# A schedule change in the last block of a hybrid transformer kernel: scan rows, row parts, scan factors and the last pass

## Chip, core and metric

The kernel runs on one core of one Trainium2 chip. The metric is device time in microseconds (us) of one execution.

## What is computed

The input is x (4 sequences of 512 rows, 256 wide, float32). Eight layers are added to it one after the other. The last three of them are the block in question:

```python
x = x + ffn(layernorm(x))        # silu(x@w_gate) * (x@w_up), the 2 largest of 4 kept, @ w_down
x = x + scan_layer(layernorm(x))
x = x + ffn(layernorm(x))        # the same weights again
# scan_layer, per sequence:
ct = concat([shifted_by_one_row(x), x], -1)
xv = sigmoid(relu(ct @ W_act.T)); re, im = pairs of xv
m = cummax(sqrt(re*re + im*im)); re, im = re / m, im / m
re, im = associative_scan(complex_multiply, (re, im))       # along the 512 rows
out = (stack(re, im) @ W_val.T) * sigmoid(relu(ct @ W_rec.T)) ** 4
```

The feed-forward has 1024 inner columns, worked in chunks of 128 (FC = 8 chunks a pass, B = 4 sequences of NT = 4 tiles of 128 rows).

## The kernel before

The whole block is one function, `feed_forward_and_scan`, with one program for each engine (`@block.tensor`, `@block.scalar`, `@block.vector`, `@block.gpsimd`, `@block.sync`). Engines meet only through semaphores, and each one works through its own list in the order in which it is written.

The work is laid out in slots n = 0 to 72. There are PASSES = 8 passes (feed-forward of the four sequences, then the second feed-forward of the four) of 8 chunks: 64 chunks in slots 0 to 63. In slot n

- TensorE computes `chunk(n)` (12 products: gate, L1735, and up, L1741), then `down(n - 7)` (products with w_down, L1751, summed in two banks of PSUM over a pass), then the jobs of `pe_at[n]`;
- ScalarE computes silu of chunk n (L1859), then the magnitude of chunk n - 1 (L1845), then the jobs of `act_at[n]`. The magnitude of a chunk whose number divides by four waits until VectorE has compared the four before (`ge_done`);
- VectorE does `dve_first[n]`, then `product(n)` (L2015), then a part of the two-of-four selection of a group of four chunks (`select`: part 0, the comparisons, L2024; part 1, the counts, L2030 to L2034; part 2, the masking, L2039, after which `sel_done` lets `down` start on the group), then `dve_at[n]`. The parts fall in slots with n mod 4 = 0, 1, 2; `down` of a new group is in a slot with n mod 4 = 3;
- GpSimd does `pool_at[n]`, the normalising of x (L1877, L1882).

A pass p ends with `added(p)` = 8(p + 1) + 7: ScalarE copies the sum of the down products from PSUM (`down_sum`, L1815) in the slot before it, and VectorE adds that to x (L2047). The scan of sequence b then begins at slot s = 15, 23, 31, 39 (`scan_from(b)`):

- s: VectorE adds and takes the moments, GpSimd normalises ("s");
- s+1: TensorE transposes the normalised rows (`row`, L1681, after `down`), ScalarE copies them to `xs` (L1777);
- s+2: TensorE computes "act" (L1690) when both copies are there, ScalarE relu, tanh, square (L1785 to L1792);
- s+3, s+4: sum of squares, running maximum, root (ScalarE, L1810), reciprocal (`invert`, L1933), `divide` (L1940, two instructions that read z with a stride and write the factors `zz`), first `level` of the scan;
- s+5, s+6: TensorE "rec" (L1699), ScalarE relu, tanh and two squares; s+5 to s+10: VectorE levels, `tree` steps, `fill` (L1953 to L1957);
- s+10: ScalarE copies `totals` (L1821, L1822) when the last tree step is done; s+11: TensorE "out" (L1710); s+13, s+14: VectorE multiplies and adds to x (L1981, L1984), takes moments for the second feed-forward; s+15: its rows ("f") are transposed.

A row of the feed-forward ("f") is cut into a high part (copied by ScalarE, L1775) and a low part (subtracted by VectorE after that copy, L1903, in `dve_at`). Only then is its bank of PSUM free. These rows are in slots 4, 12, 20 and 30, 38, 46, 54. The transposes, act, rec and out products share banks 6 and 7 in turn (`Turns`).

Because the scans are 8 slots apart, slot s+2 of a scan is slot s+10 of the one before. Where two jobs of ScalarE fall in one slot, they stand in the order in which the loop over b appends them: `totals` of b - 1 first, then the jobs of b.

SyncE stores each sequence to `out` when its last add is done (L1666).

Of the kernel before, what the change touches and what calls it, by code (L numbers as in the profile page):

```python
# [19 lines left out]
ALU = mybir.AluOpType  # L20
# [3 lines left out]
P = 128  # L24
B = 4
# [1519 lines left out]
def feed_forward_and_scan(nc, name, g, raw, w_down, scan, out):  # L1545
# [20 lines left out]
    def scan_from(b):  # L1566
        return added(b)

    pe_at, act_at, pool_at, dve_at, dve_first = ([[] for _ in range(SLOTS)] for _ in range(5))
    for p in range(1, B):  # L1570
        pe_at[FC * p - 4] += [("row", "f", p, c) for c in range(DC)]
        act_at[FC * p - 4] += [("row", "f", p, c) for c in range(DC)]
        dve_at[FC * p - 4] += [("row", "f", p, c) for c in range(DC)]
        pool_at[FC * p - 6].append(("normalise", "f", p))
    dve_at[0].append(("stats", "rest"))
    for p in range(PASSES):
        act_at[added(p) - 1].append(("sum", p))
        dve_first[added(p)].append(("add", p))
    for b in range(B):
        s = scan_from(b)  # L1580
        dve_first[s].append(("stats", "s", b))
        pool_at[s].append(("normalise", "s", b))
        pe_at[s + 1] += [("row", "s", b, c) for c in range(DC)]
        act_at[s + 1] += [("row", "s", b, c) for c in range(DC)]
        pe_at[s + 2] += [("act", b, 0), ("act", b, 1)]
        act_at[s + 2] += [("act", b, 0), ("act", b, 1), ("square", b)]
        dve_at[s + 3] += [("sum", b), ("peak", b)]
        act_at[s + 3].append(("root", b))
        dve_first[s + 4].append(("invert", b))
        dve_at[s + 4] += [("divide", b), ("level", b, 1)]  # L1590
        pe_at[s + 5].append(("rec", b, 0))
        act_at[s + 5].append(("rec", b, 0))
        dve_at[s + 5].append(("level", b, 2))
        pe_at[s + 6].append(("rec", b, 1))
        act_at[s + 6].append(("rec", b, 1))
        dve_at[s + 6].append(("level", b, 3))
        dve_at[s + 7] += [("level", b, i) for i in (4, 5, 6)]
        dve_at[s + 8] += [("level", b, 7)] + [("tree", b, d) for d in TREE[:2]]
        dve_at[s + 9] += [("tree", b, d) for d in TREE[2:5]]
        dve_at[s + 10] += [("tree", b, d) for d in TREE[5:]] + [("fill", b)]  # L1600
        act_at[s + 10].append(("totals", b))
        pe_at[s + 11] += [("out", b, m) for m in range(2)]
        dve_first[s + 13].append(("out", b))
        dve_first[s + 14].append(("stats", "f", B + b))
        pool_at[s + 14].append(("normalise", "f", B + b))
        pe_at[s + 15] += [("row", "f", B + b, c) for c in range(DC)]
        act_at[s + 15] += [("row", "f", B + b, c) for c in range(DC)]
        dve_at[s + 15] += [("row", "f", B + b, c) for c in range(DC)]

    jobs = Turns([6, 7])  # L1610
    early = [("row", "f", 0, c) for c in range(DC)]
    for todo in [early, *pe_at]:
        for job in todo:
            jobs.take(job, "dve" if job[0] == "out" or job[:2] == ("row", "f") else "act")

    with ExitStack() as stack:  # L1616
# [35 lines left out]
        r_steps, r4_ready, act_steps = s.sem("r_steps"), s.sem("r4_ready"), s.sem("act_steps")  # L1652
        peak_ready, root_ready, inverted = s.sem("peak_ready"), s.sem("root_ready"), s.sem("inverted")
        root_steps = s.sem("root_steps")
        divided, scan_steps, filled = s.sem("divided"), s.sem("scan_steps"), s.sem("filled")
        block = stack.enter_context(nc.Block())

# [3 lines left out]

        @block.sync
        def _(sp):
            for b in range(B):
                sp.wait_ge(x_done, B + b + 1)
                sp.dma_start(out[:, NT * b:NT * (b + 1), :], x[:, NT * b:NT * (b + 1), :]).then_inc(stored, 16)  # L1666
            sp.wait_ge(stored, 16 * B)

        @block.tensor
        def _(pe):  # L1670
# [74 lines left out]
            def down(m):  # L1745
                p, j = m // FC, m % FC
                if j == 0:
                    at_least(pe, sum_done, p)
                pe.wait_ge(sel_done, m // QUAD + 1)
                for t in range(NT):  # L1750
                    last = pe.matmul(ps[:, DOWN + t // 2, (t % 2) * D:(t % 2 + 1) * D], h[:, j, t * P:(t + 1) * P], w_down[:, j, :],  # L1751
                                     start=j == 0 and t % 2 == 0, stop=j == FC - 1, skip_group_check=True)
                last.then_inc(down_done, 1)

            pe.wait_ge(g["arrived"]["scan"], g["loads"]["scan"])
            pe.wait_ge(g["arrived"]["ffn1"], g["loads"]["ffn1"])
# [2 lines left out]
            for n in range(SLOTS):  # L1759
                if n < CHUNKS:  # L1760
                    chunk(n)
                if 0 <= n - DOWN_LAG < CHUNKS:
                    down(n - DOWN_LAG)
                for job in pe_at[n]:
                    do(job)

        @block.scalar
        def _(act):
# [10 lines left out]
            def act_gate(b, part):  # L1779

                job = ("act", b, part)
                if part == 0:
                    at_least(act, divided, b)
                act.wait_ge(ready, jobs.number[job])
                act.activation(z[:, part, :], ps[:, jobs.bank[job], :], ACT.Relu).then_inc(free["act"], 1)  # L1785

            def square(b):

                cs.start(b)
                act.wait_ge(free["act"], jobs.count[("act", b, 1)])  # L1790
                cs.step(act.activation(z[:, :, :], z[:, :, :], ACT.Tanh, scale=0.5))
                act.activation(sq[:, :, :], z[:, :, :], ACT.Square, bias=halfone[:, 1:2]).then_inc(sq_ready, 1)  # L1792

            def rec_gate(b, m):

# [28 lines left out]
            def do(job):  # L1824
# [4 lines left out]
                    down_sum(*a)  # L1829
                elif kind == "root":  # L1830
                    root(*a)
                elif kind == "totals":
                    totals(*a)
                elif kind == "act":
# [61 lines left out]
        def _(dve):  # L1896
# [33 lines left out]

            def invert(b):
                dve.wait_ge(root_ready, b + 1)
                dve.reciprocal(sq[:, 0, :], sq[:, 1, :]).then_inc(inverted, 1)  # L1933

            def divide(b):
                at_least(dve, totals_done, b)
                dve.wait_ge(inverted, b + 1)
                inverse = sq[:, 0, :].rearrange("p (n s) -> p s n", s=S1)
                for k in range(2):
                    last = dve.scalar_tensor_tensor(zz[:, k, :, :], z[:, k, :].rearrange("p (n s) -> p s n", s=S1), 1.0, inverse,  # L1940
                                                    ALU.add, ALU.mult)
                last.then_inc(divided, 1)
                cx.start(b)
                dve.wait_ge(divided, b + 1)

# [96 lines left out]
                    dve.sem_inc(sel_done, 1)  # L2042

            def add_to_x(p):
                dve.wait_ge(sum_done, p + 1)
                xb = x[:, NT * (p % B):NT * (p % B + 1), :]
                dve.tensor_tensor(xb, xb, dsum[:, :, :].rearrange("p k (t d) -> p (k t) d", t=2), ALU.add).then_inc(x_done, 1)  # L2047
# [15 lines left out]
            for n in range(SLOTS):  # L2063
                for job in dve_first[n]:
                    do(job)
                if n < CHUNKS:
                    product(n)
                q, part = n // QUAD - 1, n % QUAD
                if 0 <= q < CHUNKS // QUAD and part < 3:
                    select(q, part)  # L2070
# [190 lines left out]
```

## Time and profile before

| | us |
|---|---|
| median of three runs (lowest, highest) | 1575.55 (1574.22, 1578.85) |
| the profiled execution | 1575.52 |
| its span in the trace | 1573.7 |
| of it, the block in question (from the first row's transposes at 1138.07) | 435.6 |
| one scan period (row of one scan to row of the next, 1347.79 to 1409.69) | 61.9 |

The page gives busy time and share of each engine for the whole program. The trace gives, for a stretch of time, what each engine did, how long it idled ahead of an instruction and what released it (`[4.80 <-POOL xn L1882]` means 4.80 us of idling that ended with GpSimd's instruction of line 1882). Lines are those of the kernel. PE is TensorE, DVE VectorE, ACT ScalarE, POOL GpSimd. A granted clock of 1.00 is 2.4 GHz, 0.5 is 1.2 GHz.

### The profile page before, as it was taken

The page shows a single profiled execution, that of the slowest core. Times are in us where ns is not written, and L with a number is a line of the kernel's source. Part 1 is how long each engine was busy: PE and PEld are TensorE (multiplying, and loading weights), DVE is VectorE, ACT ScalarE, POOL GpSimd, SP SyncE. Part 2 cuts the span into 40 slices and gives each one's busy share as a digit, 9 for nine tenths or more (in the row PEclk, how much of TensorE's full clock was granted, in tenths as well). Part 3 has the DMA queues.
Part 4 walks back from the last instruction along what each step waited for, and adds up shares of the span by engine and source line. Part 5 has one row for each costly group of instructions (what it writes and reads, how often), then busy time and mean ns, then how long its engine had stood idle before and what let it go on. Part 6 is the DMA issues. An engine that isn't in the chain of part 4 may idle for free. (4 is left out here: it accounts for less than half of the span.)

```text
span 1573.7 us, 20720 instructions
## 1 busy us (share of the span) xinstructions
PE 1372.8 (87%) x7632; PEld 963.7 (61%) x7632; DVE 1074.9 (68%) x2164; ACT 623.5 (40%) x1159; POOL 341.3 (22%) x305
## 2 busy tenths in 40 slices
PE   3799899768999988999958799999789889889897
PEld 2455454357888877888843334333277668677676
DVE  5665655487687667867758566677366578888765
ACT  1254544443343233333313465666532334333221
POOL 2411100063433303433324140300021001021010
PEclk9799999989999999999977999999989899999899
DMA  5836240040000000000041431400000000000000
GB/s 129 95 46 82 28 57 2 1 156 1 1 1 1 1 1 1 1 1 1 1 76 22 84 61 27 52 2 2 1 1 0 1 1 1 1 0 1 15 14 27
DMA packets 32174, 39.05 MB, mean 25 GB/s; under 512 B 5986, under 2 KB 27210, under 8 KB 31946
## 3 DMA queue, kind: packets, MB, share of 16 engines
q1 hardware_dynamic: 32074, 37.73, 14.1%
q8 instruction: 61, 1.00, 0.3%
q14 instruction: 39, 0.32, 0.1%
HBM read 14.45 MB, written 2.10 MB: 11 GB/s over the span
## 5 line engine op out<-in xcount | busy, mean ns | idle before, releaser
L1314 DVE TENSOR_REDUCE attn_negm<-ps 128x2 f32<-128x1024 f32 (+3 forms) x256 | 255.9, 1021 | 89.9 <-PE ps L928 46.9
L1139 ACT ACTIVATE attn_probs<-ps 128x512 f32<-128x512 f32 (+3 forms) x512 | 237.1, 515 | 178.3 <-PE ps L956 99.5
L481 POOL TENSOR_TENSOR moe_h_low<-moe_h,moe_h_high 128x512 fp32r<-128x512 f32 x96 | 138.2, 1442 | 271.4 <-ACT moe_h_high L432 271.4
L948 PE MATMUL ps<-attn_qs,attn_ks 99*128 99x512 bf16 (+4 forms) x512 | 153.2, 347 | 31.2 <-ACT attn_probs L1139 19.1
L928 PE MATMUL ps<-attn_ks,attn_qs 96*128 96x512 bf16 (+4 forms) x512 | 142.1, 362 | 32.9 <-DMA attn_ks<-attn_part 22.3
L449 ACT ACTIVATE moe_silu<-ps 128x512 f32<-128x512 f32 x96 | 57.5, 599 | 234.2 <-PE ps L355 234.1
L1751 PE MATMUL ps<-sb_f_down,tail_h 128*128 128x256 f32 x512 | 123.5, 387 | 7.2 <-DVEq L2042 7.2
L948 PEld LDWEIGHTS ps<-attn_qs,attn_ks 102*128 102x128 bf16 (+1 forms) x512 | 49.1, 97 | 126.8 <-ACT attn_probs L1139 100.4
L969 PE MATMUL ps<-attn_probs,attn_va 128*32 128x512 f32 (+3 forms) x1024 | 117.7, 533 | 0.0
L1751 PEld LDWEIGHTS ps<-sb_f_down,tail_h 128*128 128x128 f32 x512 | 98.6, 194 | 24.3 <-DVEq L2042 7.3
L2015 DVE TENSOR_TENSOR tail_h<-tail_silu,ps 128x512 f32<-128x512 f32 x64 | 43.6, 682 | 84.7 <-PE ps L1741 54.1
L928 PEld LDWEIGHTS ps<-attn_ks,attn_qs 99*128 99x128 bf16 (+1 forms) x512 | 40.0, 101 | 93.1 <-issue 46.5
L1859 ACT ACTIVATE tail_silu<-ps 128x512 f32<-128x512 f32 x64 | 38.2, 597 | 110.3 <-PE ps L1735 110.2
L384 PE MATMUL ps<-f_down_high,moe_h_high 128*128 128x256 f32 x256 | 74.6, 291 | 3.7 <-POOL moe_h_low L481 3.7
L504 DVE TENSOR_TENSOR moe_h<-moe_silu,ps 128x512 f32<-128x512 f32 x64 | 43.4, 686 | 48.7 <-PE ps L362 33.4
L384 PE MATMUL ps<-f_down_high,moe_h_low 128*128 128x256 f32 x256 | 72.7, 284 | 0.0
L384 PE MATMUL ps<-f_down_low,moe_h_high 128*128 128x256 f32 x256 | 72.4, 283 | 0.0
L432 ACT ACTIVATE moe_h_high<-moe_h 128x512 fp32r<-128x512 f32 x96 | 60.0, 625 | 18.6 <-DVE moe_h L504 18.1
L1735 PE MATMUL ps<-tail_xh,tail_gate_high 128*128 128x512 f32 x128 | 63.3, 494 | 3.4 <-DVE tail_xl L1903 3.4
L2024 DVE TENSOR_TENSOR tail_ge<-tail_mag 128x1536 bf16<-128x1536 f32 (+2 forms) x48 | 55.8, 1219 | 0.7 <-ACT tail_mag L1845 0.7
L384 PEld LDWEIGHTS ps<-f_down_high,moe_h_high 128*128 128x128 f32 x256 | 48.7, 190 | 5.6 <-issue 4.1
L1735 PE MATMUL ps<-tail_xl,tail_gate_high 128*128 128x512 f32 x128 | 52.0, 406 | 0.0
(336 smaller groups left out, 3238.8 us busy)
## 6 DMA issues: line engine op xcount, KB each, us to landing
attn_qs<-attn_part SPq DMA_DIRECT2D x96, 128.0 KB, 4.7
attn_ks<-attn_part SPq DMA_DIRECT2D x48, 128.0 KB, 7.2
out_x<-x SPq DMA_DIRECT2D x4, 512.0 KB, 2.6
x<-in_x SPq DMA_DIRECT2D x1, 1536.0 KB, 13.4
attn_ks<-attn_part SPq DMA_DIRECT2D x24, 64.0 KB, 4.8
moe_raw<-in_f_gate SPq DMA_DIRECT2D x2, 512.0 KB, 6.7
moe_raw<-in_f_up SPq DMA_DIRECT2D x2, 512.0 KB, 7.9
moe_raw<-in_f_down SPq DMA_DIRECT2D x2, 512.0 KB, 8.7
```

The lines of the kernel that those rows point to most:

```text
L384: last = pe.matmul(ps[:, bank + t // 2, (t % 2) * D:(t % 2 + 1) * D], hp[:, j % RING, t * P:(t + 1) * P], wp[:, jw, :], start=j == 0 and t ...
L432: act.activation(hc.high[:, n % RING, :], h[:, n % RING, :], ACT.Copy).then_inc(high_done, 1)
L449: act.activation(sg[:, j % 2, :], ps[:, 2 * (j % 2), :], ACT.Silu).then_inc(silu_done, 1)
L481: pool.tensor_tensor(hc.low[:, j % RING, :], h[:, j % RING, :], hc.high[:, j % RING, :], ALU.subtract).then_inc(low_done, 1)
L928: last = pe.matmul(ps[:, 2 * (n % 2) + k, 0:width1(qt)], qs[0:ROWS1, b % 2, hd, qt * P:(qt + 1) * P], ks[0:ROWS1, b % 2, hd % KH, 0:width1 ...
L948: last = pe.matmul(ps[:, SC + k, 0:width2(kt)], ks[0:ROWS2, b % 2, hd % KH, kt * P:(kt + 1) * P], qs[0:ROWS2, b % 2, hd, T - width2(kt):T] ...
L969: last = pe.matmul(ps[SLOT * j:SLOT * (j + 1), CTX, T - width2(kt):T], va[:, b % 2, kt, hd % KH, :], pr[:, s3 % RING, j, 0:width2(kt)], st ...
L1139: act.activation(pr[:, s2 % RING, j, 0:n], ps[:, SC + k, 0:n], ACT.Exp, scale=HD ** -0.5).then_inc(exp_done, 1)
L1314: dve.tensor_reduce(m, ps[:, 2 * half:2 * half + 2, 0:width1(qt)], AX, ALU.max, negate=True).then_inc(r1_free, 1)
L1735: last = pe.matmul(ps[:, bank, :], wp[:, c, j * P:(j + 1) * P], xp[:, p % 2, c, :], start=c == 0 and k == 0, stop=c == DC - 1 and k == 2)
L1751: last = pe.matmul(ps[:, DOWN + t // 2, (t % 2) * D:(t % 2 + 1) * D], h[:, j, t * P:(t + 1) * P], w_down[:, j, :], start=j == 0 and t % 2 ...
L2024: c.do(dve.tensor_tensor(ge[:, first:first + n, :], mag[:, lo, :].unsqueeze(1).broadcast_to([P, n, T]), mag[:, lo + 1:4, :], ALU.is_ge))
```

## The change

Four edits, all in this block:

1. The transposes of a scan's rows move from slot s+1, behind `down`, to slot s+2, between `chunk` and `down` (a new list, `pe_between`). ScalarE's copies of them move from `act_at[s + 1]` to `act_at[s + 2]`.
2. VectorE's subtraction of the low part of feed-forward rows moves ahead of the selection part in its slot (`dve_middle`).
3. The factors of the scan are spread by ScalarE: after the root, `spread` writes z + 1, re-ordered, to `zz`; VectorE writes the reciprocal re-ordered, and `divide` is one multiplication in place of two instructions.
4. The last pass: the down products of its last four chunks run by halves (first the two tiles of one bank, then of the other); VectorE adds each half from PSUM to x, without ScalarE's copy, and SyncE stores each half by itself.

```diff
--- before.py
+++ after.py
@@ -1566,26 +1566,27 @@
     def scan_from(b):
         return added(b)
 
-    pe_at, act_at, pool_at, dve_at, dve_first = ([[] for _ in range(SLOTS)] for _ in range(5))
+    pe_between, pe_at, act_at, pool_at, dve_first, dve_middle, dve_at = ([[] for _ in range(SLOTS)] for _ in range(7))
     for p in range(1, B):
         pe_at[FC * p - 4] += [("row", "f", p, c) for c in range(DC)]
         act_at[FC * p - 4] += [("row", "f", p, c) for c in range(DC)]
-        dve_at[FC * p - 4] += [("row", "f", p, c) for c in range(DC)]
+        dve_middle[FC * p - 4] += [("row", "f", p, c) for c in range(DC)]
         pool_at[FC * p - 6].append(("normalise", "f", p))
     dve_at[0].append(("stats", "rest"))
     for p in range(PASSES):
-        act_at[added(p) - 1].append(("sum", p))
+        if p < PASSES - 1:
+            act_at[added(p) - 1].append(("sum", p))
         dve_first[added(p)].append(("add", p))
     for b in range(B):
         s = scan_from(b)
         dve_first[s].append(("stats", "s", b))
         pool_at[s].append(("normalise", "s", b))
-        pe_at[s + 1] += [("row", "s", b, c) for c in range(DC)]
-        act_at[s + 1] += [("row", "s", b, c) for c in range(DC)]
+        pe_between[s + 2] += [("row", "s", b, c) for c in range(DC)]
+        act_at[s + 2] += [("row", "s", b, c) for c in range(DC)]
         pe_at[s + 2] += [("act", b, 0), ("act", b, 1)]
         act_at[s + 2] += [("act", b, 0), ("act", b, 1), ("square", b)]
         dve_at[s + 3] += [("sum", b), ("peak", b)]
-        act_at[s + 3].append(("root", b))
+        act_at[s + 3] += [("root", b), ("spread", b)]
         dve_first[s + 4].append(("invert", b))
         dve_at[s + 4] += [("divide", b), ("level", b, 1)]
         pe_at[s + 5].append(("rec", b, 0))
@@ -1605,11 +1606,11 @@
         pool_at[s + 14].append(("normalise", "f", B + b))
         pe_at[s + 15] += [("row", "f", B + b, c) for c in range(DC)]
         act_at[s + 15] += [("row", "f", B + b, c) for c in range(DC)]
-        dve_at[s + 15] += [("row", "f", B + b, c) for c in range(DC)]
+        dve_middle[s + 15] += [("row", "f", B + b, c) for c in range(DC)]
 
     jobs = Turns([6, 7])
     early = [("row", "f", 0, c) for c in range(DC)]
-    for todo in [early, *pe_at]:
+    for todo in [early, *(between + after for between, after in zip(pe_between, pe_at))]:
         for job in todo:
             jobs.take(job, "dve" if job[0] == "out" or job[:2] == ("row", "f") else "act")
 
@@ -1652,6 +1653,7 @@
         r_steps, r4_ready, act_steps = s.sem("r_steps"), s.sem("r4_ready"), s.sem("act_steps")
         peak_ready, root_ready, inverted = s.sem("peak_ready"), s.sem("root_ready"), s.sem("inverted")
         root_steps = s.sem("root_steps")
+        spread_done, half_done, half_added = s.sem("spread_done"), s.sem("half_done"), s.sem("half_added")
         divided, scan_steps, filled = s.sem("divided"), s.sem("scan_steps"), s.sem("filled")
         block = stack.enter_context(nc.Block())
 
@@ -1661,10 +1663,14 @@
 
         @block.sync
         def _(sp):
-            for b in range(B):
+            for b in range(B - 1):
                 sp.wait_ge(x_done, B + b + 1)
                 sp.dma_start(out[:, NT * b:NT * (b + 1), :], x[:, NT * b:NT * (b + 1), :]).then_inc(stored, 16)
-            sp.wait_ge(stored, 16 * B)
+            for half in range(2):
+                sp.wait_ge(half_added, half + 1)
+                t0 = NT * (B - 1) + NT // 2 * half
+                sp.dma_start(out[:, t0:t0 + NT // 2, :], x[:, t0:t0 + NT // 2, :]).then_inc(stored, 16)
+            sp.wait_ge(stored, 16 * (B + 1))
 
         @block.tensor
         def _(pe):
@@ -1747,10 +1753,24 @@
                 if j == 0:
                     at_least(pe, sum_done, p)
                 pe.wait_ge(sel_done, m // QUAD + 1)
+                if p == PASSES - 1 and j >= QUAD:
+                    if j == QUAD:
+                        last_quad()
+                    return
                 for t in range(NT):
                     last = pe.matmul(ps[:, DOWN + t // 2, (t % 2) * D:(t % 2 + 1) * D], h[:, j, t * P:(t + 1) * P], w_down[:, j, :],
                                      start=j == 0 and t % 2 == 0, stop=j == FC - 1, skip_group_check=True)
                 last.then_inc(down_done, 1)
+
+            def last_quad():
+
+                for half in range(2):
+                    for j in range(QUAD, FC):
+                        for i in range(2):
+                            t = 2 * half + i
+                            last = pe.matmul(ps[:, DOWN + half, i * D:(i + 1) * D], h[:, j, t * P:(t + 1) * P], w_down[:, j, :],
+                                             start=False, stop=j == FC - 1, skip_group_check=True)
+                    last.then_inc(half_done, 1)
 
             pe.wait_ge(g["arrived"]["scan"], g["loads"]["scan"])
             pe.wait_ge(g["arrived"]["ffn1"], g["loads"]["ffn1"])
@@ -1759,6 +1779,8 @@
             for n in range(SLOTS):
                 if n < CHUNKS:
                     chunk(n)
+                for job in pe_between[n]:
+                    do(job)
                 if 0 <= n - DOWN_LAG < CHUNKS:
                     down(n - DOWN_LAG)
                 for job in pe_at[n]:
@@ -1779,8 +1801,6 @@
             def act_gate(b, part):
 
                 job = ("act", b, part)
-                if part == 0:
-                    at_least(act, divided, b)
                 act.wait_ge(ready, jobs.number[job])
                 act.activation(z[:, part, :], ps[:, jobs.bank[job], :], ACT.Relu).then_inc(free["act"], 1)
 
@@ -1790,6 +1810,11 @@
                 act.wait_ge(free["act"], jobs.count[("act", b, 1)])
                 cs.step(act.activation(z[:, :, :], z[:, :, :], ACT.Tanh, scale=0.5))
                 act.activation(sq[:, :, :], z[:, :, :], ACT.Square, bias=halfone[:, 1:2]).then_inc(sq_ready, 1)
+
+            def spread(b):
+                at_least(act, filled, b)
+                act.activation(zz[:, :, :, :], z[:, :, :].rearrange("p k (n s) -> p k s n", s=S1), ACT.Identity,
+                               bias=halfone[:, 1:2]).then_inc(spread_done, 1)
 
             def rec_gate(b, m):
 
@@ -1829,6 +1854,8 @@
                     down_sum(*a)
                 elif kind == "root":
                     root(*a)
+                elif kind == "spread":
+                    spread(*a)
                 elif kind == "totals":
                     totals(*a)
                 elif kind == "act":
@@ -1930,16 +1957,14 @@
 
             def invert(b):
                 dve.wait_ge(root_ready, b + 1)
-                dve.reciprocal(sq[:, 0, :], sq[:, 1, :]).then_inc(inverted, 1)
+                dve.reciprocal(sq[:, 0, :].rearrange("p (s n) -> p n s", s=S1),
+                               sq[:, 1, :].rearrange("p (n s) -> p n s", s=S1)).then_inc(inverted, 1)
 
             def divide(b):
-                at_least(dve, totals_done, b)
+                dve.wait_ge(spread_done, b + 1)
                 dve.wait_ge(inverted, b + 1)
-                inverse = sq[:, 0, :].rearrange("p (n s) -> p s n", s=S1)
-                for k in range(2):
-                    last = dve.scalar_tensor_tensor(zz[:, k, :, :], z[:, k, :].rearrange("p (n s) -> p s n", s=S1), 1.0, inverse,
-                                                    ALU.add, ALU.mult)
-                last.then_inc(divided, 1)
+                factors = zz[:, :, :, :].rearrange("p k s n -> p k (s n)")
+                dve.tensor_tensor(factors, factors, sq[:, 0, :].unsqueeze(1).broadcast_to([P, 2, T]), ALU.mult).then_inc(divided, 1)
                 cx.start(b)
                 dve.wait_ge(divided, b + 1)
 
@@ -2042,6 +2067,14 @@
                     dve.sem_inc(sel_done, 1)
 
             def add_to_x(p):
+                if p == PASSES - 1:
+                    for half in range(2):
+                        dve.wait_ge(half_done, half + 1)
+                        t0 = NT * (B - 1) + NT // 2 * half
+                        xb = x[:, t0:t0 + NT // 2, :]
+                        dve.tensor_tensor(xb, xb, ps[:, DOWN + half, :].rearrange("p (t d) -> p t d", t=2),
+                                          ALU.add).then_inc(half_added, 1)
+                    return
                 dve.wait_ge(sum_done, p + 1)
                 xb = x[:, NT * (p % B):NT * (p % B + 1), :]
                 dve.tensor_tensor(xb, xb, dsum[:, :, :].rearrange("p k (t d) -> p (k t) d", t=2), ALU.add).then_inc(x_done, 1)
@@ -2065,6 +2098,8 @@
                     do(job)
                 if n < CHUNKS:
                     product(n)
+                for job in dve_middle[n]:
+                    do(job)
                 q, part = n // QUAD - 1, n % QUAD
                 if 0 <= q < CHUNKS // QUAD and part < 3:
                     select(q, part)
```

## Rows read from the trace of the kernel before

**Rows 1.** The page, part 1: busy us (share), instructions.

```profile
PE 1372.8 (87%) x7632; PEld 963.7 (61%) x7632; DVE 1074.9 (68%) x2164; ACT 623.5 (40%) x1159; POOL 341.3 (22%) x305
```

**Rows 2.** Window, slots 30 to 33: us, busy PE PEld DVE ACT POOL, clock, DMA, GB/s.

```profile
1333.20:1362.70 29.50, 24.70 (x97) 17.85 (x95) 28.13 (x72) 8.61 (x17) 3.55 (x5) 0.94 0.00 0
```

**Rows 3.** Windows of TensorE alone: us, busy (count), granted clock, DMA share, GB/s.

```profile
1253.50:1259.70 6.20, 6.20 (x16) 0.53 0.00 0
...
1264.35:1267.60 3.25, 3.25 (x17) 1.00 0.00 0
...
1347.80:1351.50 3.70, 3.70 (x14) 0.54 0.00 0
...
1354.80:1361.30 6.50, 6.50 (x18) 1.00 0.00 0
...
1483.50:1488.90 5.40, 5.40 (x15) 0.59 0.00 0
```

**Rows 4.** Timeline, slots 30 to 33: start us, us, engine, line, op [idle <-releaser].

```profile
1333.84 2.49 DVE L2039 SCALAR_TENSOR_TENSOR tail_h<-tail_count,tail_h 128x512 f32<-128x512 bf16 x4
...
1334.47 1.08 ACT L1775 ACTIVATE tail_xh<-ps 128x512 fp32r<-128x512 f32 x2
...
1347.79 1.75 PE L1681 MATMUL ps<-sb_ident,xn 128*128 128x128 f32 x8 [4.80 <-POOL xn L1882]
...
1353.08 1.89 PE L1751 MATMUL ps<-sb_f_down,tail_h 128*128 128x256 f32 x8
...
1354.80 7.03 PE L1690 MATMUL ps<-tail_xs,sb_s_act 128*128 128x512 f32 x16
...
1358.77 0.44 ACT L1821 ACTIVATE tail_zt<-tail_zz 128x128 f32<-128x128 f32 x1 [5.76 <-DVE tail_zz L1957]
```

**Rows 5.** Timeline, slot 25.

```profile
1292.89 7.03 PE L1690 MATMUL ps<-tail_xs,sb_s_act 128*128 128x512 f32 x16
...
1296.83 0.44 ACT L1821 ACTIVATE tail_zt<-tail_zz 128x128 f32<-128x128 f32 x1 [5.87 <-DVE tail_zz L1957]
```

**Rows 6.** Timeline, slots 16 and 17.

```profile
1212.78 5.27 POOL L1882 TENSOR_SCALAR xn<-x,tail_ns_minus,tail_ns_rstd 128x256 f32<-128x256 f32 x4
...
1218.20 1.86 PE L1681 MATMUL ps<-sb_ident,xn 128*128 128x128 f32 x8 [2.88 <-POOL xn L1882]
...
1225.22 7.03 PE L1690 MATMUL ps<-tail_xs,sb_s_act 128*128 128x512 f32 x16
```

**Rows 7.** Timeline, slots 19 and 20.

```profile
1241.63 3.35 DVE L1933 RECIPROCAL tail_sq<-tail_sq 128x512 f32<-128x512 f32 x1 [0.70 <-ACT tail_sq L1810]
...
1245.45 2.10 DVE L1940 SCALAR_TENSOR_TENSOR tail_zz<-tail_z,tail_sq 128x512 f32<-128x512 f32 x2
...
1252.75 1.29 DVE L1903 TENSOR_TENSOR tail_xl<-ps,tail_xh 128x512 fp32r<-128x512 f32 x2
...
1253.50 6.56 PE L1699 MATMUL ps<-sb_s_rec,tail_xs 128*128 128x256 f32 x16 [6.98 <-DVE tail_xl L1903]
```

**Rows 8.** Timeline, slots 4 and 7.

```profile
1159.16 1.09 ACT L1775 ACTIVATE tail_xh<-ps 128x512 fp32r<-128x512 f32 x2 [0.68 <-PE ps L1681]
...
1170.69 3.58 PE L1751 MATMUL ps<-sb_f_down,tail_h 128*128 128x256 f32 x8 [2.96 <-DVEq L2042]
```

**Rows 9.** Timeline of TensorE, slots 50, 54 and 55.

```profile
1483.47 5.91 PE L1710 MATMUL ps<-sb_s_val,tail_zt 128*128 128x256 f32 x16 [7.86 <-DVEq L1974]
...
1509.60 1.06 PE L1681 MATMUL ps<-sb_ident,xn 128*128 128x128 f32 x8 [2.35 <-POOL xn L1882]
...
1513.28 1.89 PE L1751 MATMUL ps<-sb_f_down,tail_h 128*128 128x256 f32 x8
```

**Rows 10.** Timeline of the end; below it the page's part 6, the stores.

```profile
1568.43 1.02 ACT L1815 ACTIVATE tail_dsum<-ps 128x1024 f32<-128x1024 f32 x1 [17.84 <-PE ps L1751]
...
1569.49 1.23 DVE L2047 TENSOR_TENSOR x<-x,tail_dsum 128x1024 f32<-128x1024 f32 x1 [10.06 <-ACT tail_dsum L1815]
...
out_x<-x SPq DMA_DIRECT2D x4, 512.0 KB, 2.6
```

## Prediction

> **What bounds the kernel now.** Only the last stage is touched, from 1138 us to the end. I read the page first: TensorE is the busiest engine [rows 1]. Then the waits of this stage, which name what TensorE waited for: the normalised rows of the scan, four times, by 2.88 us to 4.8 us, once 6.98 us for a row's low part, once 7.86 us for the scan's result [rows 4, 6, 7, 9]. Then the timeline of one scan period (slots 30 to 34) on all engines. It shows two chains. TensorE is dense from the "act" products of one scan to the down products of slot 31. VectorE is dense from the product of slot 30 to the end of the scan's tree in slot 33: in that stretch of 29.5 us it is busy 28.13 us [rows 2], and its one remaining gap lies behind the stretch. So a period (61.9 us) is a TensorE part and a VectorE part laid end to end, and a TensorE stall in slots 31 to 33 costs nothing extra as long as VectorE's chain ends later. The third thing to see is the clock: after 2.35 us of idling the granted clock stayed at its upper level, after 2.88 us and more TensorE restarted at the lower one (1.2 GHz), and the clock came back later [rows 3, 4, 6, 7, 9].
>
> All my times are those of before, moved by a sum that I keep for each place.
>
> **Row parts ahead of the selection, slot 4.** VectorE now waits for ScalarE's two copies (start 1159.16) before it subtracts and selects; both subtractions and the 3.5 us of comparisons then end near 1164.7, and the next product starts about 0.5 us later than before. VectorE is dense from there to the down product that TensorE waits for [rows 8]: **+0.5 us**. (Bounds 0 to +1.) In slot 12 the same move costs VectorE about 2.2 us, which its waits for TensorE up to slot 15 absorb, but for 0.9 us that pass into the first scan's normalise.
>
> **First scan (slots 15 to 22).** Its row waits 2.88 us for GpSimd, restarts at the low clock, and "act" starts at 1225.22, 7.0 us after the row's start [rows 6]. Now the gate and up products of slot 17 (2.9 us: row and chunk together 3.68 in [rows 9], the row 0.8) come first. GpSimd's four take 5.27 us in part beside comparisons and start 0.9 us later, so the row starts near 1218.9, with about 1.0 us of idling left and the clock up; row 1.0 and down 1.7 [rows 4] put "act" at 1221.6: **-3.6 us**. ScalarE has nothing queued ahead of this scan's copies but a magnitude whose comparisons end at 1217.9. Here a rule speaks against the row's 1218.9. Trainium skill, "SBUF — State Buffer", "SBUF: two separate sides": VectorE with two SBUF inputs and GpSimd exclude each other for whole instructions. The slow 5.27 us agrees; by the rule in full the row would start up to 0.9 us later and this term would be -2.7 us.
>
> **Slot 20.** TensorE waits 6.98 us for the low part, which stands behind the comparisons, and then runs 16 products in 6.2 us that take 3.3 at the upper clock [rows 3, 7]. Two edits help. The two divisions of 2.10 us become one instruction over 1024 elements, 1.22 us by the add of that size [rows 7, 10]: 0.9 us earlier. And the subtractions no longer stand behind 3.5 us of comparisons. The low part's first half is done at 1245.35 in times that are already 3.6 us earlier, TensorE is there at 1242.7: 2.65 us of idling instead of 6.98, **-4.3 us**. 2.65 lies between 2.35 (clock kept) and 2.88 (lost); I take lost, at the price of the other short stalls (about 1.6 us: 3.7 us at 0.54 in [rows 3]) in place of 2.9: **-1.3 us** (bounds 0 and -2.9). ScalarE's "spread" (1.15 us or so, a pass over 1024 elements; the copy of that size takes 1.02 [rows 10]; up to twice that, since it reads with a stride) lies beside the 3.35 us reciprocal [rows 7] and delays only the next silu, which is done before VectorE wants it; if it took 2.3 us, under 1 us of VectorE time, which the shorter division pays back. The permuted reciprocal I take as unchanged (0 to +1).
>
> **Second scan, slot 25: the step that decides.** ScalarE's list for slot s+2 already begins with the "totals" of the scan before, because that scan's list entries (its s+10 is this s+2) are appended first. In before, the two row copies stand one slot earlier, ahead of it. Now they stand behind it. Totals waits for the last tree level on VectorE: it starts at 1296.83, having waited 5.87 us [rows 5]. Nothing in the change makes VectorE's dense chain reach it sooner. TensorE cannot begin "act" before both copies are there. So: totals 1296.83, its second part 0.35, two copies 1.25, 0.1 of signalling: "act" at 1298.5 instead of 1292.89: **+5.6 us**. Row and down products are done at about 1288.5, so TensorE idles some 10 us and restarts at the low clock. In before, "act" ran at the full clock, 6.5 us [rows 3, 4]. The price of a restart was 2.9 us after 6.98 idle and 2.3 after 7.86 (5.6 us in place of 3.3) [rows 3, 9]; I take 2.6: **+2.6 us** (bounds 1.6, the short stalls, and 6.5, the whole of "act" at half speed).
>
> **Third and fourth scans (slots 30 to 34, 38 to 42).** The same, and one thing more. In slots 30 and 38 the row parts of the feed-forward now stand before the selection's last part. VectorE waits for ScalarE's copies (start 1334.47), where before it selected from 1333.84 [rows 4]. The subtractions end at 1336.4 and the selection of 2.5 us at 1338.9, so the down product of slot 31 waits 2.4 us, and the dense VectorE chain behind is 1.27 us later. TensorE's 2.4 us is not an addition: it idles later in any case. The row starts at 1347.79+1.27, and "act" is at 1358.77+1.27+0.35+1.25+0.1 = 1361.7 instead of 1354.80: +6.95, and 2.6 for the clock [rows 4]: 9.55, twice **+19.1 us**. Behind "act" the order is TensorE's until the product of slot 38, as before, with VectorE lagging it by 2.5 us of slack, so the delay passes on whole.
>
> **The rest.** Slot 46 has the same 1.27 us, and slot 50 waits for the end of that VectorE chain [rows 9]: **+1.3**. In slot 54 the selection, put behind the copies, would end 2.5 us after them, but GpSimd, which normalised beside that selection, is less disturbed: row at about 1508.3 instead of 1509.60, down product at 1513.5 instead of 1513.28: **+0.2** (bounds -1 and +1.5) [rows 9]. At the end ScalarE's 1.02 us copy goes, VectorE's add falls from 1.23 to 0.7 us: -1.6; the last store carries half of 512 KB, which saves between nothing and half of the 2.6 us that 512 KB took to land; I take 0.5, nearer to nothing, because no shorter store stands in the trace: **-2.1 us** [rows 10]. The products themselves are as many, in another order, behind the same wait.
>
> **Sum:** +0.5 -3.6 -4.3 -1.3 +5.6 +2.6 +19.1 +1.3 +0.2 -2.1 = **+18.0 us**, on the profiled execution's 1575.5 us, which is also the median of the three runs: **1593.5 us**.
>
> **Rivals.**
> (a) *TensorE does not wait behind totals*: the change does what it looks like. For it: the four row stalls are real, and each shrinks by a chunk. Then scan two gains 4.2 (stall 3.6 and clock 1.6, less 1.0), scans three and four 2.9 each (6.5 less 2.4 and 1.15), and the sum is -19.3: 1556 us. This is the case on the other side; it needs totals to be ready before 1288.6 in place of 1296.83, 8 us sooner, and [rows 5, 4] show it late twice by the same amount. Chance 7%.
> (b) *Only the magnitude's comparisons hold the copies up* (ready at 1290.1, act at 1292.0, clock lost): scan two +0.7, scans three and four +2.0 each, in all -4.6: 1571 us. It needs the copies ahead of totals in ScalarE's list. Chance 5%.
> (c) *The low clock lasts through the whole of "act"* after the longer idling: 6.5 in place of 2.6 us three times, +11.7: 1605 us. The idle times of 10 us are longer than any in this stage; against it, the price did not grow from 6.98 to 7.86 us of idling. Chance 7%.
> The forecast has 81%.
>
> **Range.** Terms open downwards: slot 20 (-1.6), clock (-1.0 three times), slot 54 and small ones (-2), the VectorE chain lag (-1 three times): about -9. Upwards: slot 20 and GpSimd (+2.5), clock (+1 to +2 three times), +1.5 for slot 54: +8. So 1585 to 1601; (c) lies above, (a) and (b) below, together 19%. A difference of 0.3% (4.7 us) is about what a measurement of this kernel can tell. Faster: (a) and a part of (b), 8%; within 0.3%: the rest of (b) and a forecast whose terms all fall low, 5%; slower 87%.
>
> **What would show it.** In the trace of after: ScalarE's copies to the scan's xs start right behind the totals in slots 25, 33 and 41 and not in slot 17; TensorE idles about 10 us ahead of "act" three times, released by ScalarE, with the row transposes no longer waiting more than 1.2 us; "act" runs partly at the lower clock; the low-part wait ahead of "rec" falls from 6.98 to about 2.7 us; down products of slots 31 and 39 wait 2.4 us; from the last product to the end is 2 us shorter. If the period of scans two to four is still about 62 us or less, the step on totals is wrong, and with it the sign.

## Result and profile after

| | before | after |
|---|---|---|
| median of the runs (lowest, highest), us | 1575.96 (1574.22, 1578.85), 4 runs | 1598.32 (1592.22, 1604.78), 4 runs |
| ratio to before, 95% interval | | 1.0138 (1.0108 to 1.0169) |
| profiled execution: span, us | 1573.7 | 1602.9 |
| of it the changed block (first row's transposes to the end), us | 435.6 | 455.8 |

The change made the kernel slower by 1.4%, 22 us, with an interval of 17 to 27. The profiled execution of after is the slowest of its four: its span is 29.2 us longer, of which 20.2 lie in the changed block and 9.0 ahead of it, in code that is the same in both kernels (1147.06 against 1138.07 at the block's first transposes). Differences between kernels are taken inside the block, in each kernel from its own start. The rows themselves give times from the start of the execution.

The page of after, part 1, then three lines of the waits of this block (who waited for whom, us in total, times, longest):

```profile
PE 1389.3 (87%) x7632; PEld 970.0 (61%) x7632; DVE 1070.0 (67%) x2161; ACT 630.7 (39%) x1162; POOL 339.7 (21%) x305
```

```profile
PE ps L1696 <- ACT tail_xs L1799: 27.8, 3, 9.6
...
PE ps L1761 <- DVEq L2067: 12.5, 6, 3.6
...
PE ps L1687 <- POOL xn L1909: 2.6, 3, 0.9
```

The waits for normalised rows (up to 4.80 us in [rows 4]) are down to 2.6 us in all. In their place TensorE waits three times, 27.8 us in all, for ScalarE's copies, ahead of "act". Slots 24 and 25 and 30 to 33 in the timeline of after (start, us, engine, line, op, idling and releaser), to be laid beside [rows 4, 5]:

```profile
1299.36 0.44 ACT L1846 ACTIVATE tail_zt<-tail_zz 128x128 f32<-128x128 f32 x1 [5.94 <-DVE tail_zz L1982]
...
1299.69 1.07 ACT L1799 ACTIVATE tail_xs<-ps 128x512 f32<-128x512 f32 x2
...
1300.86 9.47 PE L1696 MATMUL ps<-tail_xs,sb_s_act 128*128 128x512 f32 x16 [9.61 <-ACT tail_xs L1799]
...
1344.69 1.09 ACT L1797 ACTIVATE tail_xh<-ps 128x512 fp32r<-128x512 f32 x2
...
1345.32 1.29 DVE L1930 TENSOR_TENSOR tail_xl<-ps,tail_xh 128x512 fp32r<-128x512 f32 x2 [1.18 <-ACT tail_xh L1797]
...
1346.52 2.49 DVE L2064 SCALAR_TENSOR_TENSOR tail_h<-tail_count,tail_h 128x512 f32<-128x512 bf16 x4
...
1349.21 2.99 PE L1761 MATMUL ps<-sb_f_down,tail_h 128*128 128x256 f32 x8 [2.26 <-DVEq L2067]
...
1359.93 1.03 PE L1687 MATMUL ps<-sb_ident,xn 128*128 128x128 f32 x8
...
1360.81 1.89 PE L1761 MATMUL ps<-sb_f_down,tail_h 128*128 128x256 f32 x8
...
1370.25 0.44 ACT L1846 ACTIVATE tail_zt<-tail_zz 128x128 f32<-128x128 f32 x1 [6.00 <-DVE tail_zz L1982]
...
1370.58 1.06 ACT L1799 ACTIVATE tail_xs<-ps 128x512 f32<-128x512 f32 x2
...
1371.75 9.87 PE L1696 MATMUL ps<-tail_xs,sb_s_act 128*128 128x512 f32 x16 [9.05 <-ACT tail_xs L1799]
```

Read the second part from the bottom. "act" (L1696) starts at 1371.75 after 9.05 us of idling, released by the copies at 1370.58. These begin right behind the totals (L1846, 1370.25), which had themselves waited 6.00 us for VectorE. The rows that they copy had been transposed at 1359.93 without a wait. Further up, VectorE takes the low part (L1930, with 1.18 us of idling) ahead of the selection, and the down product of slot 31 waits 2.26 us.

The slots 17 to 20, 50, 54 and the end of after:

```profile
1229.91 1.06 PE L1687 MATMUL ps<-sb_ident,xn 128*128 128x128 f32 x8 [0.79 <-POOL xn L1909]
...
1232.54 7.03 PE L1696 MATMUL ps<-tail_xs,sb_s_act 128*128 128x512 f32 x16
...
1248.82 2.26 ACT L1816 ACTIVATE tail_zz<-tail_z,tail_halfone 128x1024 f32<-128x1024 f32 x1
...
1253.02 0.69 DVE L2040 TENSOR_TENSOR tail_h<-tail_silu,ps 128x512 f32<-128x512 f32 x1 [0.71 <-ACT tail_silu L1886]
...
1253.63 1.22 DVE L1967 TENSOR_TENSOR tail_zz<-tail_zz,tail_sq 128x1024 f32<-128x1024 f32 x1
...
1257.14 5.41 PE L1705 MATMUL ps<-sb_s_rec,tail_xs 128*128 128x256 f32 x16 [3.32 <-DVE tail_xl L1930]
...
1513.94 5.33 PE L1716 MATMUL ps<-sb_s_val,tail_zt 128*128 128x256 f32 x16 [6.64 <-DVEq L1999]
...
1543.20 1.97 PE L1761 MATMUL ps<-sb_f_down,tail_h 128*128 128x256 f32 x8 [1.39 <-DVEq L2067]
...
1589.56 10.22 PE L1771 MATMUL ps<-sb_f_down,tail_h 128*128 128x256 f32 x32 [3.50 <-DVEq L2067]
...
1596.37 0.69 DVE L2075 TENSOR_TENSOR x<-x,ps 128x512 f32<-128x512 f32 x1 [6.92 <-PE ps L1771]
...
1599.82 0.69 DVE L2075 TENSOR_TENSOR x<-x,ps 128x512 f32<-128x512 f32 x1 [2.77 <-PE ps L1771]
```

The row of the first scan waits 0.79 us ([rows 6]: 2.88), "rec" 3.32 us ([rows 7]: 6.98). ScalarE's spread (L1816) takes 2.26 us, and the product at 1253.02 waits for the silu behind it. The single division (L1967) takes 1.22 us. The last 16 down products take 10.22 us; in before they took 8.86.

Granted clock of TensorE in after (stretch, us, busy and count, clock, DMA share, GB/s), at "act" of scans two and three, and one period of all engines:

```profile
1300.90:1309.70 8.80, 8.80 (x15) 0.73 0.01 2
...
1371.80:1381.00 9.20, 9.20 (x15) 0.70 0.00 0
```

```profile
1359.90:1431.00 71.10, 59.80 (x241) 45.92 (x240) 52.91 (x117) 25.40 (x36) 8.35 (x10) 0.90 0.00 1
```

In these two scans "act" ran at a mean clock of 0.73 and 0.70 of 2.4 GHz ([rows 3]: 1.00), so part of it at the lower level. The period, from row to row, is 71.2 us, against 61.9. VectorE is busy in 52.91 of them.

### The profile page after: what moved, and what is told of

Its sections match the earlier page's. It is cut to its first block and busy times, and to the rows that moved or that the text cites. A ratio compares the mean times of both kernels' runs of the same rounds, so it can differ in the third digit from the quotient of the medians.

```text
span 1602.9 us, 20720 instructions
## 1 busy us (share of the span) xinstructions
PE 1389.3 (87%) x7632; PEld 970.0 (61%) x7632; DVE 1070.0 (67%) x2161; ACT 630.7 (39%) x1162; POOL 339.7 (21%) x305
## 5 line engine op out<-in xcount | busy, mean ns | idle before, releaser
L1761 PE MATMUL ps<-sb_f_down,tail_h 128*128 128x256 f32 x480 | 116.8, 388 | 12.5 <-DVEq L2067 12.5
L1761 PEld LDWEIGHTS ps<-sb_f_down,tail_h 128*128 128x128 f32 x480 | 91.8, 193 | 29.1 <-issue 11.2
L1696 PE MATMUL ps<-tail_xs,sb_s_act 128*128 128x512 f32 x64 | 36.4, 734 | 27.8 <-ACT tail_xs L1799 27.8
L1872 ACT ACTIVATE tail_mag<-tail_h 128x512 f32<-128x512 f32 x64 | 40.1, 627 | 38.5 <-DVEq L2052 27.6
```

## Experiments

Each kernel is read in two ways: by the ratio of its time to that of before, with a 95% interval, and by the length of the changed block in its profile, which is 435.6 us in before. The block's start varies between 1134 and 1151 us over the profiles of kernels that are the same up to there, so the block's length is the sharper measure. It comes from a single trace of each kernel. Up to slot 16 of the block, where many of these kernels do the same work, their traces agree within 0.6 us, and a smaller difference of block length is not taken as an effect.

**Which part carries the loss.** The move of the rows alone, and everything but that move.

```diff
 # row_alone, against before
-        pe_at[s + 1] += [("row", "s", b, c) for c in range(DC)]
-        act_at[s + 1] += [("row", "s", b, c) for c in range(DC)]
+        pe_between[s + 2] += [("row", "s", b, c) for c in range(DC)]
+        act_at[s + 2] += [("row", "s", b, c) for c in range(DC)]
```

> Of the change only the move of the scan's row transposes (and of ScalarE's copies with them, behind totals). Theory (the copies stand behind totals in ScalarE's queue): scan one gains about 3.4 us, the wait of 6.98 us in slot 20 stays, scan two loses about 7.9 us and scans three and four about 8.2 us each, in all +21 us against before; TensorE idles about 9.5 us ahead of act three times. Rival (the loss comes from the row parts ahead of the selection and from the spread on ScalarE): this part alone gains, four shortened row waits, about -15 us.

> The change without the move of the scan's rows: row parts ahead of the selection, spread by ScalarE and last pass by halves. Theory: slot 4 costs 0.4 to 1.8 us, slot 20 gains 4 to 5, each dense VectorE chain of scans three and four is 1.3 us longer and moves the row wait by as much, the end gains 1 to 2: in all about -3 us (-6 to +1). Rival (these edits carry the loss): +10 us or more.

row_alone: ratio 1.0111 (1.0063 to 1.0159), block 452.9 us, +17.3. The wait ahead of "act" is there three times (9.61, 9.68, 9.67 us) and slot 20 is as in before (6.96 us). all_but_row: ratio 0.9982 (0.9960 to 1.0004), block 432.6 us, -3.0. The move carries the loss; the other edits do not. The expected +21 was 3.6 us too high: the first scan gave back 4.4 us in place of 3.4, the restart in slot 20 was 1.2 us cheaper than in before behind the same wait, and scan three lost 6.9 us in place of 8.2. The whole, +20.2, is 5.9 us more than the two added, and 4.6 us of this lie in scans three and four. There the restarts of "act" cost 2.8 and 3.0 us in after, against 1.5 and 2.9 in row_alone, which is 1.5 us of it. The rest goes with the row parts, which put 1.3 us each (an estimate of the prediction) into VectorE's chain, on which the copies now hang; no run separates that share.

**What holds the copies up.** Two orders of ScalarE's list in slot s+2, all else as in after.

```diff
 # copies_before_totals, against after
-        act_at[s + 2] += [("row", "s", b, c) for c in range(DC)]
+        act_at[s + 2] = [("row", "s", b, c) for c in range(DC)] + act_at[s + 2]
 # copies_first, against after
-        act_at[s + 2] += [("row", "s", b, c) for c in range(DC)]
+        act_between[s + 2] += [("row", "s", b, c) for c in range(DC)]   # done ahead of magnitude(n - 1)
```

> The whole change, but in slot s+2 ScalarE's two row copies stand ahead of totals; they still stand behind the magnitude, which waits for the comparisons. Theory: TensorE's idling ahead of act falls from 9 to about 3.5 us in scans two to four; scan two +0.7, three and four +2.0 each, scan one as in the change (-6.5), end -0.8: in all about -2 us against before. Rival (totals is not what holds the copies up): as slow as the change, +20 us.

> The whole change, but in slot s+2 ScalarE's two row copies stand ahead of the magnitude and of totals. Theory: TensorE does not idle ahead of act any more; the relu of act's first part still stands behind totals, so VectorE and ScalarE take over as the bound from there and each of scans two to four gains only 1 to 2 us against before: in all about -10 us. Rival (shifting the rows behind the chunk costs by itself): not faster than before.

"act" of the third scan in the first kernel, and ScalarE's copies, "act" and the totals of that slot in the second:

```profile
1349.13 7.11 PE L1696 MATMUL ps<-tail_xs,sb_s_act 128*128 128x512 f32 x16 [2.70 <-ACT tail_xs L1799]
```

```profile
1337.71 1.09 ACT L1800 ACTIVATE tail_xs<-ps 128x512 f32<-128x512 f32 x2 [1.20 <-PE ps L1688]
...
1339.67 7.03 PE L1697 MATMUL ps<-tail_xs,sb_s_act 128*128 128x512 f32 x16
...
1347.47 0.47 ACT L1847 ACTIVATE tail_zt<-tail_zz 128x128 f32<-128x128 f32 x1 [6.00 <-DVE tail_zz L1985]
```

copies_before_totals: 0.9988 (0.9965 to 1.0011), block 432.5 us, -3.2: one line of order takes back 23 us. The wait falls to 3.25, 2.70 and 2.64 us in scans two, three and four. copies_first: 0.9929 (0.9903 to 0.9956), block 423.5 us, -12.2: "act" follows with no wait, while the totals are as late as ever, still 6.00 us behind VectorE. So the move of the products by itself is a gain, and the place of ScalarE's copies alone turned it round: measured against all_but_row (432.6 us), the move is worth 9.1 us with the copies first and costs 23.2 us with them behind totals.

**What the idling cost at restart.** The copies stay behind totals, but TensorE computes something of no use while it waits.

```diff
 # filler, against after, ahead of act(b, 0) for b > 0, once silu and product of slot s+1 are done
+                    for _ in range(19):
+                        pe.matmul(ps[:, 2 * ((n + 1) % 2), 0:D], ident[:, :], w_act[:, 0, :], start=True, stop=True)
```

> The whole change, with 19 products of 128x128 by 128x256 (0.43 us each at the upper clock, 8.2 us) into a free bank of PSUM while TensorE waits for ScalarE's copies in scans two to four; their result is used by nothing. Theory: act starts when it did (copies behind totals), but at the upper clock: each act saves the 2.4 to 3.4 us that the restart cost, in all -7 to -9 us against the change, so about +12 us against before. Rival (the restart price is not the clock but something in act itself): as slow as the change, +20 us.

TensorE's windows over the filling products and over "act" of scan two, and that "act":

```profile
1286.40:1294.70 8.30, 8.30 (x39) 1.00 0.01 3
...
1296.10:1302.50 6.40, 6.37 (x15) 1.00 0.00 0
```

```profile
1296.13 7.11 PE L1702 MATMUL ps<-tail_xs,sb_s_act 128*128 128x512 f32 x16 [1.41 <-ACT tail_xs L1805]
```

filler: 1.0093 (1.0064 to 1.0122), block 447.2 us, 8.6 us less than after, and 7.8 of these are there by slot 42. "act" ran at a clock of 1.00 in 7.11 us (9.47 in after), and 1.41 us of idling did not cost the clock. So the price of the three restarts is measured, about 8 us. In after, "act" and what follows took 8.9, 9.3 and 9.5 us to the next chunk, against 6.5 at the full clock, which adds up to the same (8.2).

**The small edits by themselves.**

> Of the change only the row parts ahead of the selection. Theory: slot 4 costs 0.4 to 2 us, slot 20 gains about 5 (wait of 6.98 down to 3.3 and a shorter time at the low clock), down products of slots 31, 39, 47 wait 2.3 us; over the whole about -2 us (-4 to +1). Rival (the gain in slot 20 came from the shorter division): no gain, 0 to +3.

> Of the change only the spread by ScalarE and the single division. Theory: the spread takes 2.2 us on ScalarE and delays the product of slot s+4 by 0.7 us, the division saves 0.9 us; the wait of 6.98 us in slot 20 falls by 0.2 to 0.3 us, the whole moves by less than 1 us. Rival (the division shortens VectorE's chain in full): wait 6.1 us, whole -3 us.

> Of the change only the last pass by halves. Theory: -2.2 us, from the start of the last down products to the end 14.2 us in before, 12.0 here where TensorE's products take the same time. Rival (a store of half the size lands no sooner): -1.6 us.

row_parts_alone: 1.0019 (0.9995 to 1.0042), block 438.0 us, +2.4: a miss. Slot 20 did what was expected (wait 3.30 us, TensorE gains 5.0 us there). Against it, slots 7 and 8 lost 2.0 us, the first scan 0.9, scans three and four 2.4, slot 50 0.6, and the last products 1.3: they took 10.19 us behind 3.51 us of idling, where before has 8.86. spread_alone: 1.0006 (0.9985 to 1.0027), block 435.5 us, -0.1. The wait in slot 20 stayed at 6.97 us: the 0.9 us of the shorter division and the delay by the spread cancel. halves_alone: 1.0007 (0.9988 to 1.0026), not told from no change by the times; block 433.6 us, -2.0, and from the start of the last products to the end 12.0 us against 14.2. The longer and the shorter of its stores landed in 2.6 and 2.0 us, so half the bytes saved 0.6 us. The Trainium skill, "DMA: Bandwidth & Descriptors", "Anatomy of one DMA — SWDGE (gpsimd) path", has the moving of the data as bytes over 436 GB/s for DMAs that GpSimd issues; by that figure 256 KB less would save 0.6 us (an estimate). These stores are issued by SyncE, and their 0.6 us agrees.

**Towards a faster kernel.** Copies first; the row parts ahead of the selection in slot 20 alone; then also totals behind the squares (best1), then without the spread (best2).

```diff
 # copies_first_parts20, against copies_first
-        dve_middle[FC * p - 4] += [("row", "f", p, c) for c in range(DC)]
+        (dve_middle if p == B - 1 else dve_at)[FC * p - 4] += [("row", "f", p, c) for c in range(DC)]
-        dve_middle[s + 15] += [("row", "f", B + b, c) for c in range(DC)]
+        dve_at[s + 15] += [("row", "f", B + b, c) for c in range(DC)]
 # best1, against copies_first_parts20
-        act_at[s + 2] += [("act", b, 0), ("act", b, 1), ("square", b)]
+        act_at[s + 2] = [("act", b, 0), ("act", b, 1), ("square", b)] + act_at[s + 2]
```

> Copies first in slot s+2, and the row parts ahead of the selection in slot 20 alone; totals still stand ahead of act's relus. It splits the step between the kernel with the copies first (-12 us in the block) and the best one (-19 us). Theory: the row parts in the other slots cost 2 us around slot 8 and 1.3 us of VectorE chain in each of scans three and four, so this kernel reaches about -16.5 us in the block, and totals behind the squares brings the rest. Rival (the row parts elsewhere cost nothing): it stays at -12.

> Rows behind the chunk, ScalarE's order in slot s+2: silu, the two row copies, magnitude, act's relus and squares, totals last; row parts ahead of the selection in slot 20 alone; spread and halves as in the change. Theory: TensorE idles less than 2.5 us anywhere in scans two to four, relu no longer waits for totals, and VectorE's dense chain is the bound: each of these scans gains about 2.6 to 4 us against before, in all -18 us. Rival (VectorE's chain already is the bound in the kernel with the copies first): no faster than that kernel, -12 us.

> The same without ScalarE's spread (two divisions on VectorE as before). Theory: the spread's 2.2 us on ScalarE delays silu by 0.7 us and the shorter division saves 0.9 us, so the two differ by 0.2 us a scan: within 1 us of the kernel with spread. Rival (VectorE's time is the bound, and the division counts whole): 3 to 4 us slower than with spread.

copies_first_parts20: 0.9869 (0.9844 to 0.9894), block 416.6 us, -19.1. best1: 0.9866 (0.9824 to 0.9907), block 416.5. best2: 0.9868 (0.9822 to 0.9914), block 416.8. All three are 1.3% faster than before, 20 us. The row parts in the other slots cost more than expected, 6.9 us of block; the place of totals against the relus, which I had priced, is worth nothing (0.1 us), and so is the spread. A period of best1, all engines, and the one wait of VectorE for the end of its own chain:

```profile
1338.10:1397.30 59.20, 55.78 (x240) 43.55 (x240) 53.01 (x117) 25.14 (x36) 8.34 (x10) 1.00 0.00 1
```

```profile
1353.14 0.69 DVE L2043 TENSOR_TENSOR tail_h<-tail_silu,ps 128x512 f32<-128x512 f32 x1 [0.24 <-DVE tail_zt L1985]
```

59.2 us a period with TensorE busy for 55.78 of them at a clock of 1.00, and VectorE for 53.01. The product of slot 34 starts when the fill of the scan ends (0.24 us of idling, released by VectorE itself): here VectorE's chain is the bound, whatever ScalarE does first. That its length counts shows against copies_first: without the row parts in slots 30 and 38, about 1.3 us of VectorE's time each, scans three and four together are 2.5 us shorter.

## Why the prediction was right

The sign, the size (18.0 us forecast, 22 measured with 17 to 27, 20.2 in the block) and the mechanism came out: the copies stood behind totals, and one change of their order took the whole loss back. By the steps, in us within the block, from the starts of the same products in both traces:

| step | forecast | measured |
|---|---|---|
| slot 4, row parts ahead of the selection | +0.5 | +1.8 |
| first scan, row behind the chunk | -3.6 | -3.4 |
| slot 20, wait and clock | -5.6 | -4.8 |
| scan two, wait and clock | +5.6, +2.6 | +5.4, +2.4 |
| scans three and four | +19.1 | +9.4, +9.7 |
| slot 50 | +1.3 | +0.4 |
| slot 54 | +0.2 | +0.1 |
| end | -2.1 | -0.8 |
| sum | +18.0 | +20.2 |

Four rows missed by about a microsecond, two of them (slot 4 and the end) by the clock. In slot 7 the idling grew from 2.96 to 3.65 us, and slot 8 started 0.4 us later than in before. But in before the clock was 0.99 in the first 3.3 us of slot 8, and in after 0.55 in the first 3.2, which cost another 1.3 us. At the end the idling is the same (3.50 and 3.51 us) and yet the products took 10.22 us against 8.86; in the kernel with the copies first they took 8.76 behind the same wait:

```profile
1545.82 8.76 PE L1772 MATMUL ps<-sb_f_down,tail_h 128*128 128x256 f32 x32 [3.51 <-DVEq L2070]
```

Of the thirteen traces four have 10.2 us here, all of kernels with the row parts ahead of the selection in every slot; two others of that kind have 8.8 us, as have the seven that are not of that kind. Why is not shown. The price of a restart is not fixed by the length of the idling. Where the products take 8.86 us in both, the halves save 2.2 us to the end (12.0 in halves_alone, 14.2 in before), as forecast. In slot 50 the result was 1.2 us later by VectorE's chain, as forecast, but the restart behind it took 0.6 us less, after 6.64 us of idling in place of 7.86. In slot 54 GpSimd's four took 3.58 us in place of 5.05, less disturbed, as forecast. In the first scan GpSimd's four took 5.23 us, and the row started 1.0 us later than in before, counted from slot 15. The forecast had 0.7 us, and with the rule on VectorE and GpSimd that the prediction cites it would be up to 1.6; the measured start is nearer to the forecast.

Part of the close fit is luck. The 2.6 us for a restart stood for 2.4, 2.8 and 3.0 us in this trace, but in row_alone the same waits (9.61, 9.68, 9.67 us) were followed by restarts of 2.1, 1.5 and 2.9 us. And the misses of slot 4, slot 20 and the end, 3.4 us in all, are in part made up by slot 50.

In slot 20 the mis-sized term is the spread: 2.26 us where 1.15 was taken, "up to twice that" being the bound. It delayed a product by 0.7 us, and the wait was 3.32 us, not 2.65. The 0.9 us of the shorter division, which the sum counted, is not there: the wait is 3.30 us in row_parts_alone and 3.34 in best2, both without spread and single division. TensorE then ran partly at the lower clock, 1.8 us longer than at the upper. Whether the clock would have been lost after 2.65 us, as the prediction took it, was not tested here.

The rivals. (a), no wait behind totals, fell with the trace of after; the kernel with the copies first shows that its condition was one line away, with 12 us rather than 19. By the steps, scan two gained 4.3 us, as this rival had it. Scans three and four gained 0.8 and 1.7 us in place of 2.9 each, and slots 4 and 50 cost 1.5 and 1.7 us more than forecast. With the row parts taken out of all slots but 20, the gain is 19.1. (b) is the kernel with the copies before totals, forecast at -4.6 and measured at -3.2 in the block. (c) fell: after 9.05 to 9.61 us of idling the restart cost 2.4 to 3.0 us, and the longest wait, 9.68 us in row_alone, was followed by the cheapest, 1.5 us.

What stays open: why the block starts between 1134 and 1151 us in profiles of kernels that are the same up to there (9.0 us in the profiled pair). Nothing was run on it.

## What to carry to other kernels

When a job moves to a later slot, it moves behind everything that the other engines' lists already hold in that slot; read the whole list, from other iterations too, and look for an entry that waits on the engine with the latest chain. A consumer's copy belongs right behind its producer, ahead of work that nobody waits for yet. And moving work ahead on an engine that runs without a gap (here the row parts on VectorE) puts its wait for input into that engine's chain: it paid in the one slot where another engine waited for it, and cost 6.9 us in the others, the clock lost in slot 8 among it.

## What the runs showed of the hardware

- A pass of ScalarE over 1024 elements that reads with a stride of 8 elements (the spread) took 2.20 and 2.26 us in after; passes of that size that read in order took 1.01 to 1.15 us. They compute other functions, and no run has the spread's function without the stride, so that the stride is the cause is argued, not shown.
- VectorE's reciprocal took 3.36 us with its output re-ordered (a stride of 64 elements) and 3.35 without.
- The length of one idling does not tell the clock behind it. In after, the down products of slots 31, 39 and 47 waited 2.26, 2.25 and 2.25 us; the granted clock behind the first was 0.64, behind the second 0.75, behind the third 1.00. In all_but_row a row (slot 40) waited 3.63 us and ran at 1.00. In copies_before_totals "act" took 7.11 us behind 2.70 us of idling (scan three) and 8.80 us behind 2.64 (scan four). The prediction's reading, kept after 2.35 us and lost after 2.88, rested on too few rows. The windows of TensorE behind these waits, of after and then of all_but_row:

```profile
1349.20:1352.00 2.80, 2.79 (x9) 0.64 0.00 0
...
1420.50:1422.90 2.40, 2.40 (x9) 0.75 0.00 0
...
1491.90:1496.00 4.10, 4.07 (x18) 1.00 0.00 0
```

```profile
1414.40:1418.00 3.60, 3.60 (x20) 1.00 0.00 0
```

That row of all_but_row, and the "act" of scan four of copies_before_totals:

```profile
1414.38 1.06 PE L1687 MATMUL ps<-sb_ident,xn 128*128 128x128 f32 x8 [3.63 <-POOL xn L1909]
```

```profile
1411.20 8.80 PE L1696 MATMUL ps<-tail_xs,sb_s_act 128*128 128x512 f32 x16 [2.64 <-ACT tail_xs L1799]
```

- What a restart at the lower level cost "act", "rec" and "out" products varied from 1.5 to 3.0 us (8.0 us to the next chunk in scan three of row_alone, 9.5 in scan four of after, 6.5 at the full clock), and by 1.5 us between two kernels with the same 3.5 us of idling ahead of the same last products (10.22 and 8.76 us).
